# A residual block of two 3x3 convs in fp32: the far rows' products as 64 by 64 blocks on quarters of TensorE's array, and one copy of the difference sum per join

## The chip, the cores and the metric

The kernel runs on one core of one Trainium2 chip. The metric is the device time of one launch in microseconds.

## What is computed

Input x is 32 images of 64 channels, 56 by 56, in fp32. The block is a 3x3 conv, batch norm, ReLU, a second 3x3 conv, batch norm, the input added, ReLU:

```python
out = relu(_bn(_conv3x3(x, w1, stride=1), g1, b1, m1, v1))
out = _bn(_conv3x3(out, w2, stride=1), g2, b2, m2, v2)
return relu(out + identity)
```

## The kernel before, in words

**Layout.** An image is held as row pairs: 64 channels times the two rows of a pair make 128 partitions, and along the free axis stand 28 pairs by 28 even (or odd) columns. So a 128-row matmul contracts over the channels and both rows of a pair.

**Columns.** Along the columns the conv uses a transform: even and odd columns are combined into four planes, two "inner" ones (the sum and the difference of an even and an odd column, `x_inner` for the input, `t_inner` for the hidden image) and two "outer" ones (differences of columns two apart, `x_outer` and `t_outer`). Each plane is multiplied by its own filter matrix `wmat[conv][:, i]`, i = 0 to 3. Planes 1 and 2 give the sums T1 and T2 in two PSUM banks (`SUM_T1`, `SUM_T2`). The even columns are T1 + T2 + plane 0's product, the odd ones T1 - T2 + plane 3's product (banks `EVEN`, `ODD`). So after the inner products ScalarE copies T2 to `z` (`copy_sum`, L556 to 568), once plain and once negated, VectorE adds T1 to both in one instruction into `EVEN` and `ODD` (`join`, L404), and the outer products are accumulated onto that.

**Rows.** An output pair needs input rows of two neighbouring pairs. Conv 1 makes hidden pairs that are shifted by one row (`NP` = 29 of them), conv 2 turns them back. Each product is two 128x128 matrices, `far` = 0 and 1, and three of the four 64x64 blocks of each hold a filter row, the fourth is zero (`X_BLOCKS`, `HID_BLOCKS`).

**Precision.** Each product is made in three passes of the type fp32r: hi by hi, hi by lo, lo by hi, where hi is the rounded operand (ScalarE: `high_x`, `high_hidden`) and lo the rest (VectorE: `split_x`, `split_hidden`). So one product of one half image is 2 x 3 = 6 matmuls (L702). Only for images 0 and 1 some products are one fp32 matmul on the unsplit planes (`whole_passes`, operands `w_mat`).

**PSUM.** The eight banks are two halves of the image times four banks. They serve conv 1 and conv 2 in turn, with no second set.

**Steps.** The order is written out by hand, engine by engine, and kept by semaphores. In step s TensorE does, per half, conv 1's inner products of image s and conv 2's outer products of image s-2 (part A), then, per half, conv 1's outer products of image s and conv 2's inner products of image s-1 (part B), L808 to 825. VectorE's part of a step stands from L493, ScalarE's from L632. ScalarE also adds the residual into the sum banks after conv 1's join (L543), and does the two ReLUs (L573 and L608). SyncE loads and stores, GpSimd issues the accumulating load that forms the sum plane. Steps 2 to 25 run in a hardware loop of four steps.

Of the kernel before, what the change touches and what calls it, by code (L numbers as in the profile page):

```python
# [16 lines left out]
X_BLOCKS = ((0, 0, 1, 0), (0, 1, 0, 0), (0, 1, 1, 1), (1, 0, 0, 1), (1, 0, 1, 2), (1, 1, 0, 2))  # L17
HID_BLOCKS = ((0, 0, 0, 1), (0, 0, 1, 0), (0, 1, 0, 0), (1, 0, 1, 2), (1, 1, 0, 2), (1, 1, 1, 1))
OUTER = {1: {3: 0, 0: 1}, 2: {3: 0, 0: 1}}
# [7 lines left out]
def residual_block(nc, x, w1, w2, params, out):  # L27
# [4 lines left out]
    NP = NQ + 1  # L32
# [3 lines left out]

    HALF1 = ((0, (NP + 1) // 2), ((NP + 1) // 2, NP))
    HALF2 = ((0, NQ // 2), (NQ // 2, NQ))
    MAXN = HALF1[0][1] * WQ
# [5 lines left out]
    with ExitStack() as ctx:  # L45
# [8 lines left out]
        x_outer = sb("x_outer", [P, 2, RUN])  # L54
# [5 lines left out]
        t_inner = sb("t_inner", [P, 2, NP, WQ])  # L60
        t_outer = sb("t_outer", [P, 2, NP, WQ])

        ti_hi = sb("ti_hi", [P, 2, NP, WQ], F32R)
        ti_lo = sb("ti_lo", [P, 2, NP, WQ], F32R)
        h_hi = sb("h_hi", [P, 2, 2, NP, WQ], F32R)
        h_lo = sb("h_lo", [P, 2, 2, NP, WQ], F32R)
        z = sb("z", [P, 2, 2, MAXN])
        out_sb = sb("out_sb", [P, 2, 2, (NQ // 2) * WQ])

        spare = {1: z[:].rearrange("p h s r -> p (h s r)"), 2: out_sb[:].rearrange("p h s r -> p (h s r)")}  # L70
# [15 lines left out]
        w_hi = {1: sb("w1_hi", [P, 4, 2, P], F32R), 2: sb("w2_hi", [P, 4, 2, P], F32R)}  # L86
        w_lo = {1: sb("w1_lo", [P, 4, 2, P], F32R), 2: sb("w2_lo", [P, 4, 2, P], F32R)}
# [88 lines left out]
        def double_inner_filters(eng, conv, after):  # L176

            w, mat, total = w_raw[conv], wmat[conv], w_sum[conv]
            after(eng.tensor_tensor(total, w[:, 0], w[:, 2], ALU.add))
            eng.tensor_tensor(mat[:, 2], total, w[:, 1], ALU.subtract).then_inc(prep[conv], 1)  # L180
            eng.tensor_tensor(mat[:, 1], total, w[:, 1], ALU.add).then_inc(prep[conv], 1)
# [7 lines left out]
        def high_weights(conv):  # L189

            nc.scalar.wait_ge(prep[conv], 3)
            nc.scalar.wait_ge(outer_taps[conv], 1)
            nc.scalar.activation(w_hi[conv][:], wmat[conv][:], ACT.Copy).then_inc(whi_ready[conv], 1)

        def low_weights(eng, conv):

            eng.wait_ge(whi_ready[conv], 1)
            eng.tensor_tensor(w_lo[conv][:], wmat[conv][:], w_hi[conv][:].bitcast(F32),  # L198
# [10 lines left out]
        def x_full(which, k):  # L209

            full, places = (x_outer[:], slice(0, 2)) if which == "outer" else (x_inner[:, k], slice(2, 4))
# [9 lines left out]
        def hidden_rows(half):  # L221

            return slice(0, NP) if half is None else slice(*HALF1[half])

        def hidden_parts(which, b, half=None):

            rows = hidden_rows(half)
            if which != "outer":
                i = ("t1", "t2").index(which)
                return t_inner[:, i, rows], ti_hi[:, i, rows], ti_lo[:, i, rows]  # L230
            return t_outer[:, :, rows], h_hi[:, b, :, rows], h_lo[:, b, :, rows]
# [4 lines left out]

        def splits(which, n):

            return n + 1 if which == "outer" else n
# [86 lines left out]
        def _(dve):  # L326
# [19 lines left out]

            def first_x():

                dve.wait_ge(x_in[0], 16)
                cells = runs(x_sb[:, 0], 0, XPLANE + 1).rearrange("p s (j c) -> p s j c", c=WQ + 1)  # L350
                planes = x_full("inner", 0)[0]
                nc.vector.tensor_tensor(planes[:, 1], cells[:, 1, :, 0:WQ], cells[:, 0, :, 0:WQ],  # L352
                                        ALU.subtract).then_inc(tx_ready["inner"], 1)
                nc.vector.tensor_tensor(planes[:, 0], cells[:, 0, :, 0:WQ], cells[:, 1, :, 0:WQ],  # L354
                                        ALU.add).then_inc(first_sum, 1)
                cells = x_sb[:, 0, 0:2 * XPLANE].rearrange("p (s r) -> p s r", s=2)[:, :, 0:RUN] \
                    .rearrange("p s (j c) -> p s j c", c=WQ + 1)
                nc.vector.tensor_tensor(t_outer[:, :, 0:NQ], cells[:, :, :, 0:WQ], cells[:, :, :, 1:WQ + 1],  # L358
                                        ALU.subtract).then_inc(tx_ready["outer"], 1)
# [8 lines left out]
            def difference_x(n, k):  # L368
# [3 lines left out]
                cells = runs(x_sb[:, k % XBUFS], 0, XPLANE + 1).rearrange("p s (j c) -> p s j c", c=WQ + 1)  # L372
                nc.vector.tensor_tensor(x_full("inner", k)[0][:, 1], cells[:, 1, :, 0:WQ], cells[:, 0, :, 0:WQ],  # L373
                                        ALU.subtract).then_inc(tx_ready["inner"], 1)

            def outer_x(n, k):

                if is_step(n, 2):
                    dve.wait_ge(outer[1], 4)
                wait(dve, xlo_ready["outer"], n - 2)  # L380
                cells = x_sb[:, k % XBUFS]
                nc.vector.tensor_tensor(x_outer[:], runs(cells, 0, XPLANE), runs(cells, 1, XPLANE),  # L382
                                        ALU.subtract).then_inc(tx_ready["outer"], 1)
# [10 lines left out]
            def join(conv, n, half, before):  # L394

                r0, r1 = (HALF1, HALF2)[conv - 1][half]
# [6 lines left out]
                t1 = psum[:, half, SUM_T1, 0:width].unsqueeze(1).broadcast_to((P, 2, width))  # L403
# [466 lines left out]
```

## Time and profile before

| | us |
|---|---|
| median of 3 runs | 566.07 (565.9 to 566.21) |
| the profiled execution | 565.98 |
| its span | 564.3 |
| PE busy in the span | 558.4 |
| DVE busy | 542.2 |
| ACT busy | 487.2 |
| POOL busy | 30.6 |

PE is TensorE, PEld its weight loads, DVE VectorE, ACT ScalarE, POOL GpSimd, SP SyncE. The ends of matmul records are modelled and overlap the next one, so the time that a matmul takes in a stream is the distance from its start to the next start. The same holds in small for DVE and ACT, whose records overlap the next by about 0.08 us. The engine work outside of the 32 equal steps is at both ends of the kernel.

### The profile page before, as it was taken

Reading aid. Unit: us, or ns where it says so; the run is one execution under the profiler, and the core shown is the slowest. Engines: PE = TensorE matmul, PEld = TensorE weight load, DVE = VectorE, ACT = ScalarE, POOL = GpSimd, SP = SyncE. Lnnn points to the kernel's source line nnn. Section 1 sums busy time; section 2 is a strip of 40 time slices with the busy share of each in tenths; the row PEclk is TensorE's granted clock in tenths of the full one; section 3 lists DMA queues with packets and bytes.
Section 4 is the critical chain, followed back from the end, with each engine's and each line's share of the span. In section 5 each row is a group of like instructions: output and inputs, shape, how many; then the busy total and the mean of one; then the engine's idle time right before and its main releaser. Section 6 shows DMA issues by size and latency. Waiting matters only on the chain.

```text
span 564.3 us, 8999 instructions
## 1 busy us (share of the span) xinstructions
PE 558.4 (99%) x3050; PEld 543.6 (96%) x3050; DVE 542.2 (96%) x465; ACT 487.2 (86%) x744; POOL 30.6 (5%) x41
## 2 busy tenths in 40 slices
PE   8999999999999999999999999999999999999997
PEld 4689999999999999999999999999999999999997
DVE  6999999999999999999999999999999999999974
ACT  4789889888889888898888898898898988988876
POOL 3100000000000000000000000000000000000000
PEclk9999999999999999999999999999999999999999
DMA  8655445555435554445554445554355554351013
GB/s 294 180 145 145 151 109 154 148 146 165 155 91 158 159 146 151 136 120 146 174 147 143 126 138 146 149 166 151 97 158 153 146 168 142 102 154 50 30 58 114
DMA packets 31407, 79.20 MB, mean 140 GB/s; under 512 B 2592, under 2 KB 19104, under 8 KB 31392
## 3 DMA queue, kind: packets, MB, share of 16 engines
q1 hardware_dynamic: 26784, 66.05, 32.5%
q0 software_dynamic: 4464, 12.89, 14.6%
q8 instruction: 9, 0.15, 0.1%
q10 hardware_dynamic: 144, 0.07, 0.1%
q14 instruction: 6, 0.05, 0.0%
HBM read 53.31 MB, written 25.69 MB: 140 GB/s over the span
## 4 chain that ended last, share of the span: by engine, by line
PE 96%; DVE 2%; DMA 1%; issue 0%; ACT 0%; SPq 0%
PE psum L702 96%; DMA x_sb<-x_dram 1%; DVE psum L404 0%; DVE x_lo L390 0%; DVE t_outer L358 0%; DVE x_inner L352 0%; DVE x_inner L373 0%; DVE x_inner L354 0%; DVE x_outer L382 0%; DVE w_lo L198 0%; ACT out_sb L603 0%; DVE inv L332 0%; SPq L269 0%; DVE tmp L335 0%; DVE tmp L334 0%
## 5 line engine op out<-in xcount | busy, mean ns | idle before, releaser
L702 PE MATMUL psum<-x_hi,w_hi 128*128 128x420 f32 x488 | 167.2, 343 | 0.7 <-DVE x_lo L390 0.7
L702 PE MATMUL psum<-x_lo,w_hi 128*128 128x420 f32 x488 | 166.1, 340 | 0.0
L702 PE MATMUL psum<-x_hi,w_lo 128*128 128x420 f32 x488 | 166.1, 340 | 0.0
L404 DVE TENSOR_TENSOR psum<-psum,z 128x784 f32<-128x784 f32 (+1 forms) x128 | 126.9, 991 | 4.4 <-ACT z L567 4.3
L573 ACT ACTIVATE hidden<-psum,bias,half_inv 64x56 f32<-64x56 f32 (+2 forms) x128 | 84.5, 686 | 30.8 <-PE psum L702 30.3
L702 PEld LDWEIGHTS psum<-x_hi,w_hi 128*128 128x128 f32 x488 | 91.6, 188 | 2.6 <-issue 1.5
L702 PEld LDWEIGHTS psum<-x_hi,w_lo 128*128 128x128 f32 x488 | 91.7, 188 | 0.5
L702 PEld LDWEIGHTS psum<-x_lo,w_hi 128*128 128x128 f32 x488 | 91.7, 188 | 0.4
L702 PE MATMUL psum<-h_lo,w_hi 128*128 128x392 f32 x256 | 87.3, 341 | 0.0
L702 PE MATMUL psum<-h_hi,w_hi 128*128 128x392 f32 x256 | 87.3, 341 | 0.0
L702 PE MATMUL psum<-h_hi,w_lo 128*128 128x392 f32 x256 | 87.2, 341 | 0.0
L702 PE MATMUL psum<-ti_lo,w_hi 128*128 128x392 f32 x248 | 84.5, 341 | 0.0
L702 PE MATMUL psum<-ti_hi,w_hi 128*128 128x392 f32 x248 | 84.2, 340 | 0.0
L702 PE MATMUL psum<-ti_hi,w_lo 128*128 128x392 f32 x248 | 84.0, 339 | 0.0
L543 ACT ACTIVATE psum<-x_inner 128x392 f32<-128x392 f32 x128 | 58.6, 492 | 13.8 <-DVE psum L404 13.8
L608 ACT ACTIVATE out_sb<-psum 128x784 f32<-128x784 f32 x63 | 52.1, 828 | 17.3 <-PE psum L702 17.3
L441 DVE TENSOR_TENSOR ti_lo<-t_inner,ti_hi 128x812 fp32r<-128x812 f32 (+2 forms) x64 | 59.4, 970 | 0.0
L441 DVE TENSOR_TENSOR h_lo<-t_outer,h_hi 128x1624 fp32r<-128x1624 f32 (+2 forms) x33 | 59.2, 1793 | 0.0
L433 DVE TENSOR_TENSOR t_outer<-hidden 128x1624 f32<-128x1624 f32 (+2 forms) x33 | 59.1, 1790 | 0.0
L382 DVE TENSOR_TENSOR x_outer<-x_sb 128x1624 f32<-128x1624 f32 x31 | 57.1, 1842 | 0.0
L553 ACT ACTIVATE ti_hi<-t_inner 128x812 fp32r<-128x812 f32 (+2 forms) x64 | 55.8, 875 | 0.4 <-DVE t_inner L414 0.3
L390 DVE TENSOR_TENSOR x_lo<-x_inner,x_hi 128x1568 fp32r<-128x1568 f32 x31 | 55.4, 1786 | 0.0
(66 smaller groups left out, 806.3 us busy)
## 6 DMA issues: line engine op xcount, KB each, us to landing
x_sb<-x_dram SPq DMA_DIRECT2D x32, 814.0 KB, 5.0
out_dram<-out_sb SPq DMA_DIRECT2D x63, 392.0 KB, 2.8
x_inner<-x_dram SPq DMA_DIRECT2D x31, 406.0 KB, 3.2
x_inner<-x_dram POOLq DMA_DIRECT2D x31, 406.0 KB, 5.2
out_dram<-out_sb SPq DMA_DIRECT2D x2, 196.0 KB, 2.3
z<-w_dram SPq DMA_DIRECT2D x1, 384.0 KB, 3.7
out_sb<-w_dram SPq DMA_DIRECT2D x1, 384.0 KB, 6.3
bn<-params_dram ACTq DMA_DIRECT2D x1, 68.0 KB, 3.9
```

The lines of the kernel that those rows point to most:

```text
L382: nc.vector.tensor_tensor(x_outer[:], runs(cells, 0, XPLANE), runs(cells, 1, XPLANE), ALU.subtract).then_inc(tx_ready["outer"], 1)
L390: nc.vector.tensor_tensor(x_part(x_lo, k, places), full, x_part(x_hi, k, places).bitcast(F32), ALU.subtract).then_inc(xlo_ready[which], 1)
L404: nc.vector.tensor_tensor(psum[:, half, EVEN:ODD + 1, 0:width], t1, z[:, half, :, 0:width], ALU.add).then_inc(joined[conv], 1)
L433: nc.vector.tensor_tensor(t_outer[:, :, rows], hid_cols[:, :, rows, 0:WQ], hid_cols[:, :, rows, 1:WQ + 1], ALU.subtract).then_inc(th_ready ...
L441: nc.vector.tensor_tensor(lo, full, hi.bitcast(F32), ALU.subtract).then_inc(hlo_ready[which], 1)
L543: ins = nc.scalar.activation(psum[:, half, bank, 0:width].rearrange("p (j q) -> p j q", q=WQ), x_full("inner", k)[0][:, i, j0:j1], ACT.Cop ...
L553: nc.scalar.activation(hi, full, ACT.Copy).then_inc(hhi_ready[which], 1)
L573: return nc.scalar.activation(hid_data[rows, :, pairs, 0:WQ], sums[rows], ACT.Relu, bias=bias[rows, 0:1], scale=half_inv[rows, 0:1])
L608: nc.scalar.activation(out_sb[:, half], psum[:, half, EVEN:ODD + 1, 0:(j1 - j0) * WQ], ACT.Relu).then_inc(out_ready, 1)
L702: ins = nc.tensor.matmul(sums, w[:, i, far, :], t[:, j0:j1, 0:WQ], start=not onto and at == 0, stop=at == len(todo) - 1, skip_group_check= ...
```

## The change

**Rows.** The shift is gone: hidden pairs are the same as input pairs (`NP` = 28, halves of 14 pairs for both convs, 392 columns). Of the 3x3 filter's row products of a pair, four 64x64 blocks stay within the pair and fill one 128x128 matrix without a zero (`pair_products`). Two blocks reach into a neighbour pair: each is now a matmul of its own with 64 rows and 64 columns of weights (`near_products`), on 392 columns, or 364 at the image's edge. The output rows of conv 1 are swapped within a pair (`X_BLOCKS`), so its two blocks cross from partitions 0-63 to 64-127 and back, while those of conv 2 stay in their half. `near_rows` puts conv 1's and conv 2's blocks behind each other at the end of each half of part A and of part B.

**Precision.** Pair products stay in three fp32r passes for conv 1 and for conv 2's outer planes. Conv 2's inner pair products are one fp32 matmul each, and so are all the near blocks. The splits `ti_hi`, `ti_lo` of the hidden image's inner planes and their buffers are gone; `t_inner`, `t_outer` and `x_outer` get a second buffer.

**Joins.** `copy_sum` copies T2 once. `join` is two instructions, T1 + z into `EVEN` and T1 - z into `ODD`. Conv 2's bias moves from `copy_sum` to the last ReLU. The residual is two ACT instructions of 64 partitions with 784 elements instead of two of 128 with 392. `relu_hidden` is one instruction of 784 instead of two.

```diff
-            def sum_products(conv, half, i, bank, passes, onto):
...
-                todo = [(far, t, w) for far in (whole, 1 - whole) for t, w in passes]
...
+            def pair_products(conv, half, i, bank, k, native):
...
+                if native:
+                    passes = ((plane(conv, i, k), wmat[conv][:, i, 0]),)
...
+                    passes = ((hi, w_hi[conv][:, i]), (hi, w_lo[conv][:, i]), (lo, w_hi[conv][:, i]))
+                fresh = conv == 1 and i in (1, 2)
+                for at, (t, w) in enumerate(passes):
+                    ins = nc.tensor.matmul(sums, w, t[:, r0:r1, 0:WQ], start=fresh and at == 0,
+                                           stop=at == len(passes) - 1, skip_group_check=True)
...
+            def near_products(conv, half, i, bank, k):
+
+                r0, r1 = HALVES[half]
+                for source, shift in ((0, 1), (1, -1)):
+
+                    j0, j1 = max(r0, -shift), min(r1, NQ - shift)
+                    rows = slice(source * C, source * C + C)
+                    place = 1 - source if conv == 1 else source
+                    out = slice(place * C, place * C + C)
...
+                    ins = nc.tensor.matmul(sums, wmat[conv][rows, i, 1, out],
+                                           plane(conv, i, k)[rows, j0 + shift:j1 + shift], start=False, stop=True,
+                                           skip_group_check=True)
...
+            def near_rows(half, of_inner=None, of_outer=None):
+
+                for i, bank, o, target in ((2, SUM_T2, 0, EVEN), (1, SUM_T1, 3, ODD)):
+                    if of_inner:
+                        conv, k = of_inner
+                        near_products(conv, half, i, bank, k).then_inc(inner[conv], 1)
+                    if of_outer:
+                        conv, k = of_outer
+                        ins = near_products(conv, half, o, target, k)
...
-                t1 = psum[:, half, SUM_T1, 0:width].unsqueeze(1).broadcast_to((P, 2, width))
-                nc.vector.tensor_tensor(psum[:, half, EVEN:ODD + 1, 0:width], t1, z[:, half, :, 0:width],
-                                        ALU.add).then_inc(joined[conv], 1)
...
+                for bank, op in ((EVEN, ALU.add), (ODD, ALU.subtract)):
+                    ins = nc.vector.tensor_tensor(psum[:, half, bank, 0:width], psum[:, half, SUM_T1, 0:width],
+                                                  z[:, half, 0:width], op)
+                ins.then_inc(joined[conv], 1)
...
-                for i, bank, share in ((0, SUM_T1, 0.5), (1, SUM_T2, -0.5)):
-                    ins = nc.scalar.activation(psum[:, half, bank, 0:width].rearrange("p (j q) -> p j q", q=WQ),
-                                               x_full("inner", k)[0][:, i, j0:j1], ACT.Copy, scale=share)
+                for source, target in ((slice(C, P), slice(0, C)), (slice(0, C), slice(C, P))):
+                    sums = psum[target, half, SUM_T1:SUM_T2 + 1, 0:width].rearrange("p s (j q) -> p s j q", q=WQ)
+                    ins = nc.scalar.activation(sums, x_full("inner", k)[0][source, :, j0:j1], ACT.Copy, scale=0.5)
...
-                if conv == 1:
-                    nc.scalar.activation(z[:, half, 0, 0:width], t2, ACT.Copy)
-                    ins = nc.scalar.activation(z[:, half, 1, 0:width], t2, ACT.Copy, scale=-1.0)
...
+                ins = nc.scalar.activation(z[:, half, 0:width], t2, ACT.Copy)
```

The engines' rows in the steady state. First PE, part A of the first half in the loop, before: conv 2's outer products of image s-2, whose two matrices have six passes per plane (`h_hi` and `h_lo` are the split outer planes of the hidden image).

```order
L702 MATMUL psum<-h_hi,w_hi 128x392 [waits joined2,hlo_outer]
L702 MATMUL psum<-h_hi,w_lo 128x392
L702 MATMUL psum<-h_lo,w_hi 128x392
L702 MATMUL psum<-h_hi,w_hi 128x392
L702 MATMUL psum<-h_hi,w_lo 128x392
L702 MATMUL psum<-h_lo,w_hi 128x392
L702 MATMUL psum<-h_hi,w_hi 128x392
L702 MATMUL psum<-h_hi,w_lo 128x392
L702 MATMUL psum<-h_lo,w_hi 128x392
L702 MATMUL psum<-h_hi,w_hi 128x392
L702 MATMUL psum<-h_hi,w_lo 128x392
L702 MATMUL psum<-h_lo,w_hi 128x392
```

In the changed kernel the same place has six passes for both planes (the last four stand here), and then the eight 64-row matmuls of `near_rows`, two of conv 1 (`x_inner`) and two of conv 2 (`t_outer`) in turn.

```order
L651 MATMUL psum<-h_lo,w_hi 128x392
L651 MATMUL psum<-h_hi,w_hi 128x392
L651 MATMUL psum<-h_hi,w_lo 128x392
L651 MATMUL psum<-h_lo,w_hi 128x392
L665 MATMUL psum<-x_inner,w_mat 64x392
L665 MATMUL psum<-x_inner,w_mat 64x364
L665 MATMUL psum<-t_outer,w_mat 64x392
L665 MATMUL psum<-t_outer,w_mat 64x364
L665 MATMUL psum<-x_inner,w_mat 64x392
L665 MATMUL psum<-x_inner,w_mat 64x364
L665 MATMUL psum<-t_outer,w_mat 64x392
L665 MATMUL psum<-t_outer,w_mat 64x364
```

Of the twelve passes six are left, and eight fp32 matmuls of a quarter of the array each end the half. The signal that conv 1's sums are complete now comes from among these eight.

Then DVE, before: a step of the loop from conv 2's join of the second half (image s-2) to conv 1's join of the second half (image s). L404 is the join, L390 the split of an x plane, L441 that of a hidden plane.

```order
L404 TENSOR_TENSOR psum<-psum,z 128x2x392 [waits hidden_ready,inner2,z2_ready]
L433 TENSOR_TENSOR t_outer<-hidden 128x1624 [waits hlo_outer]
L390 TENSOR_TENSOR x_lo<-x_outer,x_hi 128x1568 [waits xhi_outer]
L399 ISA
L400 ISA [waits z1_ready]
L404 TENSOR_TENSOR psum<-psum,z 128x2x420 [waits out_ready,inner1]
L441 TENSOR_TENSOR ti_lo<-t_inner,ti_hi 128x812 [waits hhi_t1]
L441 TENSOR_TENSOR ti_lo<-t_inner,ti_hi 128x812 [waits hhi_t2]
L441 TENSOR_TENSOR h_lo<-t_outer,h_hi 128x1624 [waits hhi_outer]
L399 REGISTER_ALU
L400 ISA [waits z1_ready]
L404 TENSOR_TENSOR psum<-psum,z 128x2x392 [waits out_ready,inner1]
```

The same stretch after, up to the hidden image's split; L393 is the join, L379 and L420 are the splits.

```order
L379 TENSOR_TENSOR x_lo<-x_outer,x_hi 128x1568 [waits xhi_outer]
L393 TENSOR_TENSOR psum<-psum,z 128x392 [waits hidden_ready,inner2,z2_ready]
L393 TENSOR_TENSOR psum<-psum,z 128x392
L144 REGISTER_ALU [waits hidden_ready]
L401 TENSOR_TENSOR t_inner<-hidden 128x784 [waits inner2]
L412 TENSOR_TENSOR t_outer<-hidden 128x1568 [waits outer2]
L388 ISA
L389 ISA [waits z1_ready]
L393 TENSOR_TENSOR psum<-psum,z 128x392 [waits out_ready,inner1]
L393 TENSOR_TENSOR psum<-psum,z 128x392
L406 TENSOR_TENSOR t_inner<-hidden 128x784
L420 TENSOR_TENSOR h_lo<-t_outer,h_hi 128x1568 [waits hhi_outer]
```

The split of the outer x plane moved from behind the hidden image's planes to ahead of conv 2's join, the two splits of `t_inner` are gone, the difference of the hidden columns moved behind conv 1's first join, and each join is two rows.

## Rows read from the trace of the kernel before

**Rows 1.** Section 1 of the page: busy time, share of the span, instructions.

```profile
PE 558.4 (99%) x3050; PEld 543.6 (96%) x3050; DVE 542.2 (96%) x465; ACT 487.2 (86%) x744; POOL 30.6 (5%) x41
```

**Rows 2.** Section 2 of the page: the granted clock in 40 slices.

```profile
PEclk9999999999999999999999999999999999999999
```

**Rows 3.** Windows: busy time of each engine (x instructions), 100 to 500 us.

```profile
100.00:500.00 400.00, 400.00 (x2245) 399.12 (x2244) 395.49 (x329) 354.32 (x539) 20.70 (x24) 1.00 0.50 146
```

**Rows 4.** The chain that ended last: start us, us, what.

```profile
19.22 542.00 PE psum L702 x3008
...
561.25 0.50 ACT out_sb L603
```

**Rows 5.** Timeline of DVE: start us, us, engine, line, operation, tiles, forms.

```profile
290.37 0.96 DVE L373 TENSOR_TENSOR x_inner<-x_sb 128x784 f32<-128x784 f32 x1
...
300.51 1.84 DVE L441 TENSOR_TENSOR h_lo<-t_outer,h_hi 128x1624 fp32r<-128x1624 f32 x1
302.27 0.97 DVE L404 TENSOR_TENSOR psum<-psum,z 128x784 f32<-128x784 f32 x1
303.16 1.84 DVE L382 TENSOR_TENSOR x_outer<-x_sb 128x1624 f32<-128x1624 f32 x1
304.91 1.78 DVE L390 TENSOR_TENSOR x_lo<-x_inner,x_hi 128x1568 fp32r<-128x1568 f32 x1
306.62 0.98 DVE L404 TENSOR_TENSOR psum<-psum,z 128x784 f32<-128x784 f32 x1
307.50 0.96 DVE L373 TENSOR_TENSOR x_inner<-x_sb 128x784 f32<-128x784 f32 x1
308.65 1.00 DVE L414 TENSOR_TENSOR t_inner<-hidden 128x812 f32<-128x812 f32 x1 [0.19 <-PE psum L702]
309.58 1.00 DVE L421 TENSOR_TENSOR t_inner<-hidden 128x812 f32<-128x812 f32 x1
...
341.72 0.97 DVE L373 TENSOR_TENSOR x_inner<-x_sb 128x784 f32<-128x784 f32 x1
```

**Rows 6.** Timeline of PE: twelve three-pass matmuls in the steady state.

```profile
302.15 0.34 PE L702 MATMUL psum<-ti_hi,w_hi 128*128 128x392 f32 x1
...
304.10 0.34 PE L702 MATMUL psum<-ti_lo,w_hi 128*128 128x392 f32 x1
304.28 0.34 PE L702 MATMUL psum<-x_hi,w_hi 128*128 128x392 f32 x1
```

**Rows 7.** Groups by form, PE: count | busy us, mean ns of one.

```profile
L702 PE MATMUL psum<-ti_hi,w_hi 128*128 128x392 f32 x248 | 84.2, 340 | 0.0
...
L702 PE MATMUL psum<-t_inner,w_mat 128*128 128x392 f32 x16 | 5.6, 492 | 0.0
```

**Rows 8.** Timeline of PE: fp32 matmuls without splits, early in the kernel.

```profile
26.29 2.80 PE L702 MATMUL psum<-t_inner,w_mat 128*128 128x392 f32 x8
28.92 2.71 PE L702 MATMUL psum<-x_outer,w_mat 128*128 128x392 f32 x8
```

**Rows 9.** Timeline of DVE, near the end: the 392-element forms.

```profile
550.25 0.56 DVE L414 TENSOR_TENSOR t_inner<-hidden 128x392 f32<-128x392 f32 x1
550.72 0.56 DVE L421 TENSOR_TENSOR t_inner<-hidden 128x392 f32<-128x392 f32 x1
```

**Rows 10.** Groups by form, ACT.

```profile
L543 ACT ACTIVATE psum<-x_inner 128x392 f32<-128x392 f32 x128 | 58.6, 492 | 13.8 <-DVE psum L404 13.8
L553 ACT ACTIVATE ti_hi<-t_inner 128x812 fp32r<-128x812 f32 x60 | 53.8, 897 | 0.4 <-DVE t_inner L414 0.3
L608 ACT ACTIVATE out_sb<-psum 128x784 f32<-128x784 f32 x63 | 52.1, 828 | 17.3 <-PE psum L702 17.3
L573 ACT ACTIVATE hidden<-psum,bias,half_inv 64x56 f32<-64x56 f32 x64 | 25.0, 391 | 30.4 <-PE psum L702 30.3
```

**Rows 11.** Timeline of PEld: weight loads while PE stands idle.

```profile
19.19 0.19 PEld L702 LDWEIGHTS psum<-x_hi,w_hi 128*128 128x128 f32 x1 [1.29 <-issue]
19.30 0.19 PEld L702 LDWEIGHTS psum<-x_hi,w_lo 128*128 128x128 f32 x1
```

More of the change, by code:

```diff
@@ L209, in x_full @@
         def x_full(which, k):
-            full, places = (x_outer[:], slice(0, 2)) if which == "outer" else (x_inner[:, k], slice(2, 4))
+            full, places = (x_outer[:, k % 2], slice(0, 2)) if which == "outer" else (x_inner[:, k], slice(2, 4))
             return full.rearrange("p s (j c) -> p s j c", c=WQ + 1)[:, :, :, 0:WQ], places
@@ L219, in until, with hidden_outer @@
             return (n - k % 2) * 8 + 16
[L221 to L231, printed above, removed]
+        def hidden_outer(b):
+            return t_outer[:, b], h_hi[:, b], h_lo[:, b]
         def split_of_x(which, n):
             return n - 1 if which == "outer" else n
-        def splits(which, n):
-            return n + 1 if which == "outer" else n
         def before_conv2(n):
@@ L653, in step @@
                     copy_sum(2, 0, 1)
+                    high_x("outer", 2, 2)
                     return
-                if now:
-                    high_x("outer", s, k)
-                if last:
-                    high_hidden("t1", s - 1, kl % 2)
+                if ahead:
+                    high_x("inner", s + 1, ka)
+                if there_is(s, s - 2):
+                    relu_out(s - 2, 0)
                 if now:
@@ L676, in step @@
                 if last:
-                    residual(s - 1, kl, 1)
                     copy_sum(2, s - 1, 0)
+                if ahead:
+                    high_x("outer", s + 1, ka)
                 if now:
@@ L747, in outer_products, with inner_pairs_1, outer_pairs @@
+            def inner_pairs_1(half, k, native=False):
+                for i, bank in ((2, SUM_T2), (1, SUM_T1)):
+                    pair_products(1, half, i, bank, k, native)
+            def outer_pairs(conv, n, half, k, native=False):
                 pe.wait_ge(joined[conv], 2 * n + half + 1)
                 for i, bank in ((0, EVEN), (3, ODD)):
-                    first = conv == 1 and (is_step(n, 0) or is_step(n, 1))
-                    passes = whole_passes(1, i, n) if first else passes_of(conv, i, b)
@@ L751, in outer_products, with inner_pairs_2 @@
-                    ins = sum_products(conv, half, i, bank, passes, True)
-                    if conv == 2 and half == 1 and is_step(n, N - 1):
-                        ins.then_inc(last_bank, 1)
-                if not (conv == 2 and half == 1 and is_step(n, N - 1)):
-                    ins.then_inc(outer[conv], 1)
+                    pair_products(conv, half, i, bank, k, native)
+            def inner_pairs_2(n, half, k):
+                pe.wait_ge(th_ready["t1"], n + 1)
+                pe.wait_ge(th_ready["t2"], n + 1)
+                pe.wait_ge(res_ready, 2 * n + half + 1)
+                for i, bank in ((2, SUM_T2), (1, SUM_T1)):
+                    pair_products(2, half, i, bank, k, True)
```

335 lines of the change are left out of this document (136 added, 199 removed).

## The prediction

> **What bounds the kernel now.** I read the page's first two sections, a window of the steady state, the chain, and then timelines. PE is busy for 99% of the span and DVE for 96% [rows 1], and the chain is 542.0 us of matmuls without a break, from 19.22 us to the last ReLU [rows 4]. The granted clock stays at its upper level, 2.4 GHz [rows 2, 3]. Between 100 and 500 us PE is never idle and DVE is busy 395.5 of 400 us, ACT 354.3 [rows 3]. So two engines are close to full, and ACT is not far behind. The same DVE operation starts at 290.37 and, three steps later, at 341.72 [rows 5]: a step (one image) takes 17.12 us. 32 steps are 547.8 us, and the other 16.5 us of the span lie at its ends. The profiled execution took 565.98 us, 1.7 us more than its span and 0.1 under the median, so I add 1.7 to a span.
>
> **Part 1, fewer three-pass matmuls.** Twelve of them start between 302.15 and 304.28 [rows 6]: 0.1775 us each for 392 columns. A step had 96; 36 are left (conv 1's four planes and conv 2's two outer ones, two halves, three passes). 36 x 0.1775 = 6.4 us.
>
> **Part 2, conv 2's inner pairs in fp32.** Four fp32 matmuls of 392 columns appear as eight records and take 28.92 - 26.29 = 2.63 us [rows 8], so 0.657 us each, as two records of 0.329. (Three passes would be 0.53.) Four per step: 2.6 us.
>
> **Part 3, the near blocks.** A step has four calls of `near_rows` with eight matmuls of 64 rows by 64 columns each, in fp32. The trace has no matmul on part of the array, so I bound a call. If four run at once, one in each quarter, a call is two rounds of the full-size fp32 matmul, 2 x 0.657 = 1.31 us. If none overlap it is 8 x 0.657 = 5.26 us. Cheaper than 1.31 would need a matmul to take less than its columns did in rows 8, and nothing in the program makes them fewer. I take 1.31: the two blocks of conv 1 and the two of conv 2 use the four different quarters, stand behind each other, and depend on nothing of each other. Four calls: 5.3 us.
>
> **Part 4, changing between whole array and quarters.** Eight changes a step. A three-pass matmul's record lasts 340 ns [rows 7] while the next starts after 177.5 [rows 6], so some 0.165 us of each lies over its successor. If the array has to run empty at a change, that overlap is lost: 8 x 0.165 = 1.3 us. The other end is 0. The Trainium skill, TensorEngine Tiling (Array Packing), Key Properties, says that changing the tiling mode drains TensorE. By that rule the 1.3 us are real; if it did not hold PE's sum would be 43 us lower (rival D); no row here shows a change.
>
> I take 0.165, the only size that the rows give for an emptying pipe.
>
> PE's step: 6.4 + 2.6 + 5.3 + 1.3 = **15.6 us**.
>
> **Part 5, DVE.** By distances of starts [rows 5]: x split 1.71, `x_outer` 1.75, join of 784 elements 0.89, a hidden plane of 812 elements 0.93 (0.89 for 784, by the join), and `x_inner` 0.88 (its record less 0.08). 392 elements take 0.47 from SBUF [rows 9]; I take 0.48 for them from PSUM (the joins of 784 run 0.01 longer than `x_inner` of 784). New step: `x_inner` 0.88, `x_outer` 1.75, two x splits, `t_outer` and `h_lo` of 1568 elements each 4 x 1.71, sum and difference 2 x 0.89, eight half joins 8 x 0.48 = 3.84. Together 15.1 us, where it was about 16.9 [rows 3]. The splits of `t_inner` go (-1.8), the joins grow by 0.3. DVE alone would give 32 x 15.1 + 16.5 + 1.7 = 501 us.
>
> **Part 6, ACT.** From 15.2 us a step (354.3 us over 23.4 steps [rows 3]) go two `ti_hi` of 0.90, the two short ReLUs of 0.39, and four z copies, about 0.49 each by the residual's form of the same 392 elements [rows 10]; the residual's four instructions of 784 elements are put at 0.83 (the last ReLU's 784 elements, [rows 10]) to 1.0 us instead of 0.49, +1.4 to +2.0. That leaves 12 to 12.6 us. ACT does not bound; the removed ACT work is worth nothing by itself. Smaller edits (half the weight splits at the start, the bias in the last ReLU) lie beside matmuls or DVE's start; the load requests keep their waits and only come 1.5 us closer together, with the DMA engines half busy [rows 3]. I cost them at nothing.
>
> **The sum over the whole kernel,** since one-conv calls at the ends fill only two quarters. Everything before 19.2 us stays: image 0's fp32 matmuls and near blocks have the same total as the two full matrices had (16 x 0.657 against 8 x 0.657 + 4 x 1.31). Behind it: 1116 three-pass matmuls, 198.1; 132 fp32 ones, 86.7; the equivalent of 130 near calls, 170.8; 262 changes, 43.2; together 498.8. With 19.2 ahead and the last ReLU's 0.5 the span is 518.5, and the time **520 us**.
>
> **Where it is tight.** The waits go around through the single set of PSUM banks. From the start of a step DVE now needs 0.88 + 1.71 + 0.96 = 3.55 us to finish conv 2's second join, and PE asks for it after 12 x 0.1775 + 1.31 + 0.33 = 3.77. Conv 1's first join ends at 3.55 + 0.89 + 1.71 + 0.96 = 7.1, PE asks at 7.5; the residual on ACT behind it (two of at least 0.75 by distance of starts) ends at 8.6, and PE's next inner pair asks at 7.5 + 1.07 = 8.6. Behind a late join stand DVE's splits, and on PE, behind the waiting pair, the near blocks that release both convs' sums. So a slower residual is seen at once: 0.5 us a step is 16 us. I put nothing into the point for it and 25 us into the range.
>
> **Rivals.**
>
> *A. The quarters run only two at a time (0.16).* Each fp32 matmul is two records [rows 7, 8] and the second needs the same quarter as the first. If matmuls start strictly in the order of the program, the next block's first half can only start with this block's second half: 16 records become 8 slots of 0.329, a call 2.63 us instead of 1.31. 122 two-conv calls lie behind 19.2 us: 122 x 1.31 = +160, **680 us**, slower. For it: no row shows PE starting matmuls out of order. Against: no row shows it starting two together either, so the rows are silent. The Trainium skill, TensorEngine Tiling (Array Packing), PSUM Pressure, gives another way to the same time: row tiles must not use one PSUM bank at the same time, and the two blocks of a `near_products` do write one bank (on different partitions); they would then go one after the other, beside the other conv's, which is again two at a time. The break-even for all such cases: 46 us over 122 calls, so a two-conv call with its changes of 2.0 us, where I have 1.64.
>
> *B. Nothing overlaps (0.04).* 122 x (5.26 - 1.31) = +482, and +10 from the one-conv calls: about 1010 us.
>
> *C. The weight loads set the pace of the near rows (0.05).* With PE idle two loads start 0.11 us apart [rows 11]. A call has 16 loads; at 0.11 each, if a load of 64 columns costs as much as one of 128 and cannot hide, it takes 1.76 us instead of 1.31: +55, 575 us, slower.
>
> *D. The changes cost nothing, and DVE sets the pace (0.12).* PE's step is 14.3, DVE's 15.1: 501 us. A DVE between two engines rarely runs without a gap, so some more is as likely.
>
> *E. The waits of the tight places add 0.8 to 1.4 us a step (0.14).* 545 to 565 us, with PE idle before `t_inner` or the outer pairs.
>
> **Chances.** The forecast, 505 to 545 us, has 0.48; D 0.12 and E 0.14 are faster than before as well. Within 0.2% (1.1 us, about what a measurement of this kernel can tell from no change): 0.01. Slower: A 0.16, B 0.04, C 0.05. So faster 0.74, same 0.01, slower 0.25. The range takes in D, E and C, 498 to 590 us, and leaves out A and B. For the likeliest sign alone it is 498 to 560.
>
> **What would show it.** Right: 64-row matmuls that start within some tens of ns of each other, four abreast, a call near 1.3 us, a gap of 0.1 to 0.2 us at each change; a step of 15.5 to 15.8; DVE busy 97% with eight joins of about 0.56 us; ACT near 80%. A is right if 64-row records start 0.33 us apart. C if weight loads are back to back with matmuls spaced behind them. D if the changes leave no gap and PE waits for joins. E if PE is idle ahead of `t_inner` with ACT's residual as the releaser. The forecast is wrong if a call with its changes is over 2.0 us, or if the step is over 17.1 us for any reason.

## The result and the profile after

The changed kernel takes 547.41 us (median of 4 runs, 547.39 to 547.64) against 566.0 us in the same session: a ratio of 0.967, 95% interval 0.966 to 0.969. It is 18.6 us faster. The forecast was 520 us, 46 us faster. The gain is 0.4 of that one; the time lies in the stated range, 498 to 590 us, and 2.4 us above the forecast's own 505 to 545 us.

The page, section 1, of the changed kernel, to be laid beside [rows 1]:

```profile
PE 531.8 (97%) x3454; PEld 317.6 (58%) x3454; DVE 486.0 (89%) x525; ACT 412.4 (76%) x487; POOL 30.1 (6%) x41
```

The windows view of the changed kernel, the steady state (busy time and instructions of PE, PEld, DVE, ACT, POOL; granted clock, DMA share, GB/s), to be laid beside [rows 3]:

```profile
100.00:500.00 400.00, 396.88 (x2674) 242.99 (x2674) 374.28 (x398) 317.54 (x372) 20.76 (x24) 1.00 0.51 149
```

All three engines do less. Yet no engine is full for 400 us any more: PE is idle for 3 us and DVE for 26. The length of a step is read from the timeline of DVE, from `x_outer` to `x_outer`, 21 steps apart:

```profile
99.18 1.84 DVE L344 TENSOR_TENSOR x_outer<-x_sb 128x1624 f32<-128x1624 f32 x1
...
439.30 1.84 DVE L344 TENSOR_TENSOR x_outer<-x_sb 128x1624 f32<-128x1624 f32 x1
```

340.12 / 21 = 16.20 us a step, where it was 17.12 and 15.6 was forecast. (The steps behind the hardware loop, from 26 on, are a little shorter, 16.04 us.) So 30 steps (2 to 31) cost some 17 us more than forecast, and the other 10 us lie at the ends.

The near rows do what they say. Timeline of PE in the changed kernel, part A of a first half, from its first whole-array matmul through one call of `near_rows` to the next whole-array one:

```profile
298.53 0.45 PE L651 MATMUL psum<-x_hi,w_hi 128*128 128x392 f32 x1
...
300.59 0.33 PE L651 MATMUL psum<-h_lo,w_hi 128*128 128x392 f32 x1
300.85 0.54 PE L665 MATMUL psum<-x_inner,w_mat 64*64 64x392 f32 x2
300.86 0.54 PE L665 MATMUL psum<-t_outer,w_mat 64*64 64x392 f32 x2
301.21 0.47 PE L665 MATMUL psum<-x_inner,w_mat 64*64 64x364 f32 x1
301.23 0.47 PE L665 MATMUL psum<-t_outer,w_mat 64*64 64x364 f32 x1
301.23 0.49 PE L665 MATMUL psum<-x_inner,w_mat 64*64 64x392 f32 x1
301.24 0.49 PE L665 MATMUL psum<-t_outer,w_mat 64*64 64x392 f32 x1
...
302.32 0.45 PE L651 MATMUL psum<-x_hi,w_hi 128*128 128x392 f32 x1
```

Four records start within some 0.03 us (the row marked x2 holds two of them), the next four some 0.3 us later, and so on: four rounds, sixteen records. From 300.85 to 302.32 is 1.47 us. A whole first half of part A takes 302.32 - 298.53 = 3.79 us; the forecast's terms for it (12 x 0.1775 + 1.31 + 0.33) give 3.77.

What the forecast did not have is the gap on DVE. Timeline of DVE in the changed kernel over the same stretch:

```profile
302.46 1.78 DVE L412 TENSOR_TENSOR t_outer<-hidden 128x1568 f32<-128x1568 f32 x1
304.20 1.05 DVE L393 TENSOR_TENSOR psum<-psum,z 128x392 f32<-128x392 f32 x2
305.15 0.96 DVE L406 TENSOR_TENSOR t_inner<-hidden 128x784 f32<-128x784 f32 x1
306.04 1.78 DVE L420 TENSOR_TENSOR h_lo<-t_outer,h_hi 128x1568 fp32r<-128x1568 f32 x1
308.88 1.05 DVE L393 TENSOR_TENSOR psum<-psum,z 128x392 f32<-128x392 f32 x2 [1.06 <-ACT z L531]
309.84 1.84 DVE L344 TENSOR_TENSOR x_outer<-x_sb 128x1624 f32<-128x1624 f32 x1
```

Timeline of ACT in the changed kernel beside it:

```profile
304.27 1.51 ACT L522 ACTIVATE h_hi<-t_outer 128x1568 fp32r<-128x1568 f32 x1 [0.40 <-DVE t_outer L412]
305.81 1.66 ACT L513 ACTIVATE psum<-x_inner 64x784 f32<-64x784 f32 x2
307.41 0.89 ACT L557 ACTIVATE out_sb<-psum,bias 128x784 f32<-128x784 f32 x1
308.21 0.48 ACT L531 ACTIVATE z<-psum 128x392 f32<-128x392 f32 x1
```

ACT waits for `t_outer`, rounds it, and only then makes the residual, the output ReLU of the second half and the copy of T2. DVE's second join of conv 1 waits for that copy, and everything of DVE stands behind it, the next step's `t_outer` too. From one `t_outer` back to it that is a ring. Its ACT part takes 4.42 us (from 304.27 to 308.69), and the DVE work beside it, a join, a difference and a split, only 3.62 (from 304.20 to 307.82).

### The profile page after: what moved, and what is told of

It is laid out like the page before. It is cut to its first block, busy times and chain, and to the rows that moved or that the text cites. A ratio compares the mean times of both kernels' runs of the same rounds, so it can differ in the third digit from the quotient of the medians.

```text
span 545.8 us, 9539 instructions
## 1 busy us (share of the span) xinstructions
PE 531.8 (97%) x3454; PEld 317.6 (58%) x3454; DVE 486.0 (89%) x525; ACT 412.4 (76%) x487; POOL 30.1 (6%) x41
## 4 chain that ended last, share of the span: by engine, by line
DVE 44%; PE 24%; issue 16%; ACT 13%; DVEq 1%; ACTq 0%; POOL 0%; POOLq 0%
PE psum L651 14%; DVE psum L393 12%; PE psum L665 9%; DVE x_lo L379 9%; DVE t_outer L412 8%; DVE x_outer L344 7%; ACT psum L513 6%; DVE t_inner L401 4%; ACT out_sb L557 4%; DVE x_inner L338 3%; ACT z L531 2%; PE psum L705 1%; ACT h_hi L522 1%; DVEq L144 1%; DVE h_lo L420 0%
## 5 line engine op out<-in xcount | busy, mean ns | idle before, releaser
L393 DVE TENSOR_TENSOR psum<-psum,z 128x392 f32<-128x392 f32 x256 | 133.2, 565 | 42.8 <-ACT z L531 38.9
L513 ACT ACTIVATE psum<-x_inner 64x784 f32<-64x784 f32 x128 | 105.5, 824 | 39.0 <-DVE psum L393 37.4
L651 PE MATMUL psum<-t_inner,w_mat 128*128 128x392 f32 x256 | 99.3, 510 | 7.7 <-ACT psum L513 5.9
L665 PE MATMUL psum<-t_outer,w_mat 64*64 64x392 f32 (+1 forms) x512 | 98.4, 491 | 0.0
L665 PE MATMUL psum<-x_inner,w_mat 64*64 64x392 f32 (+1 forms) x512 | 98.0, 490 | 0.0
L665 PE MATMUL psum<-x_outer,w_mat 64*64 64x392 f32 (+1 forms) x512 | 98.0, 490 | 0.0
L665 PE MATMUL psum<-t_inner,w_mat 64*64 64x392 f32 (+1 forms) x512 | 98.0, 490 | 0.0
L651 PE MATMUL psum<-x_hi,w_hi 128*128 128x392 f32 x244 | 95.9, 393 | 1.9 <-DVE psum L393 1.9
L651 PE MATMUL psum<-x_hi,w_lo 128*128 128x392 f32 x244 | 83.0, 340 | 0.0
L651 PE MATMUL psum<-x_lo,w_hi 128*128 128x392 f32 x244 | 82.8, 339 | 0.0
L420 DVE TENSOR_TENSOR h_lo<-t_outer,h_hi 128x1568 fp32r<-128x1568 f32 x32 | 57.0, 1782 | 1.6 <-ACT h_hi L522 1.6
L379 DVE TENSOR_TENSOR x_lo<-x_outer,x_hi 128x1568 fp32r<-128x1568 f32 x30 | 53.5, 1783 | 2.0 <-ACT x_hi L502 2.0
L379 DVE TENSOR_TENSOR x_lo<-x_inner,x_hi 128x1568 fp32r<-128x1568 f32 x31 | 55.3, 1783 | 0.0
```

Of the source, the lines that this page charges most:

```text
L379: nc.vector.tensor_tensor(x_part(x_lo, k, places), full, x_part(x_hi, k, places).bitcast(F32), ALU.subtract).then_inc(xlo_ready[which], 1)
L393: ins = nc.vector.tensor_tensor(psum[:, half, bank, 0:width], psum[:, half, SUM_T1, 0:width], z[:, half, 0:width], op)
L420: nc.vector.tensor_tensor(lo, full, hi.bitcast(F32), ALU.subtract).then_inc(hlo_ready["outer"], 1)
L513: ins = nc.scalar.activation(sums, x_full("inner", k)[0][source, :, j0:j1], ACT.Copy, scale=0.5)
L651: ins = nc.tensor.matmul(sums, w, t[:, r0:r1, 0:WQ], start=fresh and at == 0, stop=at == len(passes) - 1, skip_group_check=True)
L665: ins = nc.tensor.matmul(sums, wmat[conv][rows, i, 1, out], plane(conv, i, k)[rows, j0 + shift:j1 + shift], start=False, stop=True, skip_g ...
```

## Experiments

Each run is set beside the kernel before (565.7 to 565.8 us in these sessions). "Step" is the mean over 17 to 21 steps, read as above. Line numbers move by a few lines between the kernels.

**1. The near blocks conv by conv.**

```diff
-                for i, bank, o, target in ((2, SUM_T2, 0, EVEN), (1, SUM_T1, 3, ODD)):
-                    if of_inner:
+                if of_inner:
+                    for i, bank in ((2, SUM_T2), (1, SUM_T1)):
                         conv, k = of_inner
                         near_products(conv, half, i, bank, k).then_inc(inner[conv], 1)
-                    if of_outer:
+                if of_outer:
+                    for o, target in ((0, EVEN), (3, ODD)):
                         conv, k = of_outer
                         ins = near_products(conv, half, o, target, k)
-                if of_outer:
                     ins.then_inc(outer[of_outer[0]], 1)
```

> The near blocks of the two convs no longer alternate: in each call conv by conv, so at most two quarters have work at a time. Theory T (four quarters really work at once, and PE's own work sets the step): each two-conv call grows from two to four rounds of an fp32 matmul, 1.31 us; 120 calls in the steps: about +155 us, some 703 us. Rival R1 (the four abreast records are only how the profile draws them, and PE works through them at two at a time in any order): no change, 547 us. Rival R2 (DVE and ACT's ring of waits sets the step, PE has slack): less than half of T's, under 625 us.

548.26 us, step 16.21: no change. Theory T's premise, that this order leaves work for two quarters only, was wrong. Timeline of PE in this run, one call:

```profile
302.01 0.54 PE L665 MATMUL psum<-x_inner,w_mat 64*64 64x392 f32 x2
302.04 0.54 PE L665 MATMUL psum<-t_outer,w_mat 64*64 64x392 f32 x2
302.38 0.51 PE L665 MATMUL psum<-x_inner,w_mat 64*64 64x364 f32 x2
302.40 0.51 PE L665 MATMUL psum<-t_outer,w_mat 64*64 64x364 f32 x2
...
303.50 0.45 PE L651 MATMUL psum<-x_hi,w_hi 128*128 128x392 f32 x1
```

`t_outer`'s first block starts 0.03 us after `x_inner`'s, although four blocks of `x_inner` stand ahead of it in the program: a quarter that is free takes its matmul from further back. So this run does not take the four-abreast work apart. It gives rival R1's number too, and R1 stays open until run 2, which does take it apart.

**2. The near blocks of each conv behind its own pairs, in part A.**

```diff
                         inner_pairs_1(half, k)
+                        near_rows(half, (1, k), None)
...
-                        near_rows(half, (1, k) if now else None, (2, kb) if store else None)
+                        if store:
+                            near_rows(half, None, (2, kb))
```

> In part A of each half conv 1's near blocks stand directly behind conv 1's pair products, and conv 2's behind conv 2's: whole-array matmuls lie between, so only two quarters can have work, and there are 4 more changes a step. If a call of one conv takes as long as one of two convs (1.47 us from its first matmul to the next whole-array one in the changed kernel's trace) plus 0.18 us for the extra changes, PE's part A grows by 1.65 us a half: 2 x 1.65 x 30 = 99, less the 0.25 us a step that PE stands now: about 638 us. If four abreast are no faster than two, so that a one-conv call takes half: 555 us, like the run with more changes.

630.73 us, ratio 1.115 (1.113 to 1.117), step 19.02: 2.8 us more a step (638 us was expected; R1's like here was 555). Timeline of PE, a call with one conv's blocks alone:

```profile
304.41 1.53 PE L665 MATMUL psum<-x_inner,w_mat 64*64 64x392 f32 x8
305.87 0.45 PE L651 MATMUL psum<-h_hi,w_hi 128*128 128x392 f32 x1
```

Half the blocks take 1.46 us, as long as all of them. The second conv's blocks in a call are free. This is what rival A denied, shown by its price: with two quarters at work in part A alone, the kernel would be slower than before.

**3. More changes between whole array and quarters, in part A.**

```diff
-                        inner_pairs_1(half, k)
...
-                        outer_pairs(2, s - 2, half, kb)
+                        pe.wait_ge(joined[2], 2 * (s - 2) + half + 1)
...
-                        near_rows(half, (1, k) if now else None, (2, kb) if store else None)
+                        for i, bank, o, target in ((2, SUM_T2, 0, EVEN), (1, SUM_T1, 3, ODD)):
+                            if now:
+                                pair_products(1, half, i, bank, k, False)
+                            if store:
+                                pair_products(2, half, o, target, kb, False)
+                            if now:
+                                near_products(1, half, i, bank, k).then_inc(inner[1], 1)
+                            if store:
+                                ins = near_products(2, half, o, target, kb)
+                        if store:
+                            ins.then_inc(outer[2], 1)
```

> Part A of each half makes the same matmuls, but the near blocks in two lots, each behind the pair products of its own planes: 4 more changes between whole array and quarters, and 4 fewer stretches of a full length between them, per step. If a change costs the 0.165 us of the prediction and PE sets the step, 4 x 0.165 x 30 = +20 us, 567 us. If it costs 0.24 (the measured PE step of 15.9 us less 14.3, over 8 changes, less what else may be in it: an upper figure), +24 to +29, up to 576 us. If changes are free and the rest of PE's step has another cause, 547 us. If the ring of DVE and ACT sets the step, also near 547 us.

555.25 us, ratio 0.982 (0.980 to 0.984), step 16.44. Timeline of PE, the first half of part A, with four changes in it instead of two:

```profile
301.73 0.45 PE L651 MATMUL psum<-x_hi,w_hi 128*128 128x392 f32 x1
...
305.88 0.45 PE L651 MATMUL psum<-x_hi,w_hi 128*128 128x392 f32 x1
```

4.15 us against 3.79 for two changes more: 0.18 us a change. The forecast's 0.165 was right in size. The kernel grew by less (8 us instead of 20), which says that PE's own work was not what set the step of 16.20.

**4. No near blocks.**

```diff
-                    pair_products(1, half, i, bank, k, native)
+                    pair_products(1, half, i, bank, k, native).then_inc(inner[1], 1)
...
             def near_rows(half, of_inner=None, of_outer=None):
+                return
```

The other pair products raise their semaphores in the same way. The output lacks the neighbour pairs' part.

> All near blocks are left out (the output lacks each output pair's contribution from the neighbour pair), with their changes; the semaphores are raised by the pair products. PE's step is then 6.4 + 2.6 = 9.0 us. It shows the step of DVE and ACT alone. DVE's work is 15.1 us a step. If DVE can run without gaps: 32 x 15.1 + 16.5 + 1.7 = about 501 us. If the ring of waits (single set of PSUM banks) sets a floor near the measured step of 16.2 even with a fast PE: 535 to 547 us. In between: waits remain, but PE's own work is the larger part of the loss.

537.56 us. The step, from the same rows of DVE, 19 steps apart:

```profile
111.09 1.84 DVE L344 TENSOR_TENSOR x_outer<-x_sb 128x1624 f32<-128x1624 f32 x1
...
418.97 1.84 DVE L344 TENSOR_TENSOR x_outer<-x_sb 128x1624 f32<-128x1624 f32 x1
```

(418.97 - 111.09) / 19 = 16.20 us, the same as with them, though PE is now busy for 215 of 320 us (window 100 to 420). And DVE has the same gap ahead of the same join:

```profile
304.58 1.05 DVE L393 TENSOR_TENSOR psum<-psum,z 128x392 f32<-128x392 f32 x2 [1.11 <-ACT z L531]
```

So in the changed kernel DVE and ACT set the step, by their order; PE is just short of it. The 10 us that this run is faster lie at the ends. (With PE idle that often, its granted clock was 0.974 and 0.958 in the two executions, 536.53 and 538.6 us. PE does not set the step here: run 9 below, with PE as idle and a clock of 1.00 in this window, again has the step of the kernel with near blocks.)

**5. The ring shortened.** Run 4's kernel, and one of the residual's two instructions left out.

```diff
-                for source, target in ((slice(C, P), slice(0, C)), (slice(0, C), slice(C, P))):
+                for source, target in ((slice(C, P), slice(0, C)),):
```

> The changed kernel's order, without near blocks, and with one of the residual's two instructions left out (the output lacks the neighbour pairs' contributions and the input on half of the rows). The run without near blocks kept the step of 16.20 us. Theory T2 (ring: DVE t_outer, ACT rounding, two residual instructions, output ReLU, copy of T2, DVE join, and then DVE without a gap to the next t_outer): one instruction less on ACT, 0.80 us by distance of starts, takes 0.8 us from every step: 15.4 us, about 512 us. Rival (the residual lies beside the ring, which runs through the copy or the rounding alone): 16.2 us, 537 us.

513.53 us, step 15.48: 0.72 us less a step for an instruction of 0.80. The residual is in the ring. That is where the change's own form of it counts: two instructions of 64 partitions and 784 elements take 1.66 us. In a timeline of ACT before, two of 128 by 392 take 0.92:

```profile
298.81 0.92 ACT L543 ACTIVATE psum<-x_inner 128x392 f32<-128x392 f32 x2 [0.52 <-DVE psum L404]
```

Each instruction now has twice the elements on half of the partitions. What the old form would give in the changed kernel was not run.

**6. The joins alone, on the kernel before.**

```diff
+                for bank, op in ((EVEN, ALU.add), (ODD, ALU.subtract)):
+                    ins = nc.vector.tensor_tensor(psum[:, half, bank, 0:width], psum[:, half, SUM_T1, 0:width],
+                                                  z[:, half, 0, 0:width], op)
...
-                if conv == 1:
-                    nc.scalar.activation(z[:, half, 0, 0:width], t2, ACT.Copy)
-                    ins = nc.scalar.activation(z[:, half, 1, 0:width], t2, ACT.Copy, scale=-1.0)
...
+                ins = nc.scalar.activation(z[:, half, 0, 0:width], t2, ACT.Copy)
...
-                                     ACT.Relu).then_inc(out_ready, 1)
+                                     ACT.Relu, bias=bias[:, 1:2]).then_inc(out_ready, 1)
```

> The kernel before with only one part of the change: the difference sum copied once, each join as an addition and a subtraction, conv 2's bias in the last ReLU. ACT loses four copies a step (about 1.6 us by distance of starts), DVE's joins grow by 0.06 us each, four a step, so 16.9 + 0.25 = 17.15 us against a step of 17.12. Theory T (the part helps ACT only, which does not bound): 566 to 572 us. Rival: ACT's copies were on the ring of waits, so a shorter ACT gives some time back: 560 to 565 us.

566.36 us, ratio 1.0011 (1.0002 to 1.0021). Window of this run:

```profile
100.00:500.00 400.00, 400.00 (x2245) 399.11 (x2244) 400.00 (x424) 316.00 (x445) 20.71 (x24) 1.00 0.49 146
```

ACT falls from 354 to 316 us and nothing comes of it; DVE rises from 395.5 to 400. This part of the change gives no time by itself, as forecast; it makes room on ACT, which the new residual takes.

**7. ACT's order in steps 1 and N.**

```diff
+                    residual(N - 1, kl, 1)
                     high_hidden(N - 1, kl % 2)
-                    residual(N - 1, kl, 1)
...
                     high_x("inner", 2, 2)
+                    residual(0, 0, 1)
                     high_hidden(0, 0)
                     relu_hidden(1, 0)
-                    residual(0, 0, 1)
                     copy_sum(2, 0, 0)
+                    high_x("outer", 2, 2)
                     relu_hidden(1, 1)
                     copy_sum(2, 0, 1)
-                    high_x("outer", 2, 2)
```

> Only ScalarE's order in steps 1 and N is changed: in step 1 the second residual goes ahead of the hidden image's rounding and the rounding of image 2's outer x planes goes ahead of the last hidden ReLU; in step N the second residual goes ahead of the rounding. In the changed kernel's trace PE stands for 1.63 us before the second inner pairs of conv 2, 1.92 us before conv 1 of image 2, and 0.93 us in the tail. Theory (these waits are on the path that sets the end): up to 4.5 us less, 543 to 545 us. Rival: the waits only move on to the next join: no change, 547 us.

544.33 us, ratio 0.962 (0.961 to 0.964): 3.1 us of the 4.5. So about a third of the 10 us that the ends cost more was order.

**8. The ring's order in every step.** On top of run 7:

```diff
                 if last:
                     difference_hidden(s - 1, kl % 2)
-                    split_hidden(s - 1, kl % 2)
+                if ahead:
+                    outer_x(s + 1, ka)
                 if now:
                     join(1, s, 1, (2, s - 2))
+                if last:
+                    split_hidden(s - 1, kl % 2)
                 if ahead:
-                    outer_x(s + 1, ka)
                     split_x("inner", s + 1, ka)
...
                 if last:
-                    high_hidden(s - 1, kl % 2)
                     residual(s - 1, kl, 0)
...
                     copy_sum(1, s, 1)
                 if last:
+                    high_hidden(s - 1, kl % 2)
                     residual(s - 1, kl, 1)
```

The first piece is DVE's order, the second ACT's.

> The order of e5, and in every step of the loop: ScalarE makes the residual, the output ReLU and the copy of T2 ahead of the rounding of the hidden outer planes; VectorE makes the next image's x_outer ahead of conv 1's second join and the split of the hidden planes behind it. Same instructions. Theory T2 (the ring DVE t_outer, ACT rounding, residual, output ReLU, copy, DVE join sets the step at 16.2 us, as the run without near blocks showed, and DVE's gap of 1.06 to 1.11 us a step is that ring): the gap shrinks, and PE's own 15.95 us set the step: about 7 us less than e5, 536 to 539 us. Rival R3 (PE with its changes sets the step as much): less than 3 us under e5. Rival R4 (the ring only moves, for the split of the hidden planes now comes later): 547 us or more.

534.92 us, ratio 0.946 (0.944 to 0.947), step 15.86: 9.4 us under run 7 from the same instructions. The gap ahead of the join is now 0.47 us, and PE is busy for all 400 us of its window.

**9. The same order without near blocks.** Run 8's kernel with the edit of run 4.

> The order of e6 with all near blocks left out (the output lacks the neighbour pairs' contributions), so PE's step is some 9 us and the step is what DVE and ACT need. Theory T2: DVE's 15.1 us of work bound it, 15.1 to 15.4 us a step: 505 to 515 us. Rival R4 (the ring only moved): a step of 16 us or more, over 530 us.

527.62 us and a step of 15.86 again. Both theories missed: the ring had shortened by 0.35 us and still was no shorter than PE's own step. In the gap DVE waits behind `x_outer` for ACT's residual, ReLU and copy. Timeline of DVE in run 9:

```profile
314.36 1.05 DVE L393 TENSOR_TENSOR psum<-psum,z 128x392 f32<-128x392 f32 x2 [0.47 <-ACT z L533]
315.59 1.79 DVE L420 TENSOR_TENSOR h_lo<-t_outer,h_hi 128x1568 fp32r<-128x1568 f32 x1 [0.19 <-ACT h_hi L524]
```

**10. More DVE work between conv 1's two joins.** On top of run 8 the sum of the hidden columns moves behind the first join.

```diff
-                    sum_hidden(s - 1, kl % 2)
+                    dve.wait_ge(hidden_ready, 2 * (s - 1) + 2)
                     outer_hidden(s - 1, kl % 2)
                 if now:
                     join(1, s, 0, (2, s - 2))
                 if last:
+                    sum_hidden(s - 1, kl % 2)
                     difference_hidden(s - 1, kl % 2)
```

> The order of e6, and DVE's sum of the hidden columns moved behind conv 1's first join, so that DVE has 3.5 us of its own work between conv 1's two joins instead of 2.6 (the chain on ACT between them is about 3.1). Same instructions. If in e6 the ring alone sets the step of 15.86 us, it falls with the ring, to 15.5 or so: 524 to 530 us. If PE's own work of some 15.9 us sets it as well (its window of 400 us had no idle time), the time stays at 534 to 536 us.

533.52 us, ratio 0.943 (0.941 to 0.944), step 15.85 in the loop.

**11. The same order without near blocks.** Run 10's kernel with the edit of run 4.

> e10 with all near blocks left out (the output lacks the neighbour pairs' contributions): what DVE and ACT alone need a step in that order. If the move shortens the ring: 15.1 to 15.5 us a step, 505 to 518 us. If the gap only moves to another join: 15.86 us, 527 us.

501.93 us, step 15.01. The windows view of run 10:

```profile
100.00:420.00 320.00, 320.00 (x2184) 199.55 (x2188) 304.95 (x325) 256.95 (x303) 18.12 (x21) 1.00 0.52 157
```

The same window of run 11:

```profile
100.00:420.00 320.00, 226.77 (x939) 161.16 (x937) 320.00 (x342) 266.14 (x320) 18.13 (x21) 0.99 0.55 164
```

In run 11 DVE is busy for all of 320 us: its own work is 15.0 us a step, and the ring no longer adds to it. So in run 10, where PE is full, it is PE that sets the step of 15.85. Behind the loop PE is as full, and run 10's step is shorter. Timeline of DVE in run 10, four steps apart:

```profile
424.89 1.84 DVE L344 TENSOR_TENSOR x_outer<-x_sb 128x1624 f32<-128x1624 f32 x1
...
487.78 1.84 DVE L344 TENSOR_TENSOR x_outer<-x_sb 128x1624 f32<-128x1624 f32 x1
```

62.89 / 4 = 15.72 us. Run 10 is the fastest complete kernel here, 32 us under the kernel before and 14 under the changed one, with the changed one's instructions in another order.

## Why the prediction was right or wrong

*What held.* Four quarters work at once (part 3): 1.47 us for a call with its last change, and run 2 for the price of losing it. Rivals A and B are out, and so is C, by the same 1.47 us against its 1.76 without a change; weight loads of neighbouring quarters start together, as the records do (300.85 and 300.86). A change costs 0.18 us in run 3 (part 4: 0.165), so rival D is out as well. The Trainium skill, TensorEngine Tiling (Array Packing), Key Properties, has a drain at a change of mode; run 3 agrees, with 0.18 us. DVE's own step is 15.0 us in run 11 (part 5: 15.1) and the work taken off ACT is worth nothing by itself (part 6, run 6). ACT's step is 12.9 us (317.54 of 400 us), a little over the 12 to 12.6 of part 6. The rule of the same page of the Trainium skill, PSUM Pressure, that row tiles cannot use one bank at the same time, does not hold for this kernel. Timeline of PE in the changed kernel:

```profile
297.41 0.47 PE L665 MATMUL psum<-t_inner,w_mat 64*64 64x364 f32 x1
297.42 0.47 PE L665 MATMUL psum<-x_outer,w_mat 64*64 64x364 f32 x1
297.44 0.49 PE L665 MATMUL psum<-t_inner,w_mat 64*64 64x392 f32 x1
297.45 0.49 PE L665 MATMUL psum<-x_outer,w_mat 64*64 64x392 f32 x1
```

The two records of `t_inner` are the two blocks of one product. They read different halves of the partitions, write one bank on different partitions, and start 0.03 us apart; taking turns, they would need the 2.63 us a call of rival A, and it takes 1.47.

*What failed first: "I put nothing into the point for it", the waits of the tight places.* The prediction found the tight places and then took all waits as nothing, because each sum of durations just fitted PE's clock. It had left out what stands around the residual in ACT's queue. The residual does not stand directly behind conv 1's first join; the rounding `h_hi` stands ahead of it, which waits for `t_outer`. And the second join needs the copy, which stands behind the residual and the output ReLU. Counted as it stands in the order, ACT's part is 1.5 + 1.6 + 0.8 + 0.5 = 4.4 us, and DVE has only 3.6 us to put beside it. The difference, 0.8 us, and the hand-overs from DVE to ACT and back (0.07 us before 304.27, 0.19 behind 308.69) are DVE's gap of 1.06 us, and 15.1 + 1.1 = 16.2 is the step. Two busy engines that hand work to each other in fixed order have a period of their own; "PE 15.6, DVE 15.1, so 15.6" skipped it. Runs 4 and 5 show it, and runs 8 and 10 take it away: 16.20 - 15.85 = 0.35 us a step, some 10 us. Rival E had the right time (545 to 565) and the residual as a culprit, but its time is in part luck: it put 0.8 to 1.4 us of waits into each step, where they cost 0.35, and the rest of the miss came from PE's own step and the ends. Its sign is there, but small: the page has PE idle for 7.7 us ahead of `t_inner`, 5.9 of it by the residual. PE is nearly as slow as the ring, and a record's modelled end hides some 0.16 us of each wait.

*What failed second: PE's step, 15.85 instead of 15.6,* 7 us over 30 steps. One half of it is the price of a change (part 4). With 0.18 instead of 0.165 for each of the eight, PE's terms give 15.7, and run 10 has 15.72 behind the loop. The prices of parts 1 to 3 hold. Timeline of PE in run 10 there, the two fp32 pair products of a half of part B:

```profile
441.38 1.48 PE L654 MATMUL psum<-t_inner,w_mat 128*128 128x392 f32 x4
442.78 0.54 PE L668 MATMUL psum<-t_inner,w_mat 64*64 64x392 f32 x2
```

They take 1.40 us: 2 x 0.657 = 1.31 and the change into quarters, 0.09 (in part A the last whole-array matmul takes 300.85 - 300.59 = 0.26 instead of 0.1775). The other half is 0.13 us that only the steps in the loop have. In the changed kernel's loop the same two products take

```profile
311.68 1.58 PE L651 MATMUL psum<-t_inner,w_mat 128*128 128x392 f32 x4
313.19 0.55 PE L665 MATMUL psum<-t_inner,w_mat 64*64 64x364 f32 x2
```

1.51 us, and in run 10's loop one of the two pairs of a step takes 1.48. What makes them longer in the loop stays open.

*Third, the ends, 10 us.* 3.1 are waits behind ACT's order (run 7). 2.4 are the last store: the sum over the whole kernel ended with the last ReLU, but in the changed kernel that ends at 543.4 and the span at 545.8 us. It was inside the 16.5 us of the step-wise sums, and got lost when the prediction changed to the other way of summing. 0.5 are image 0: its changes were not counted, and the matmuls behind it start at 19.69 instead of 19.2. The other 4 us were not traced.

Together 10 + 7 + 10 = 27 us, which is the miss.

## What to carry to other kernels

When two engines are both near full and wait for each other, write down the ring between them, every queued instruction included, before taking the larger sum of work as the period; the sum of the durations around it is a third candidate beside the two engines. Leaving out one engine's work altogether (here PE's near rows) tells in one run which of the three sets the step. And after a change that moves work between engines, the order of the queues is worth another look: here it held back 14 us that the change had already paid for.

## What was not expected of the hardware

A free quarter of TensorE's array takes a matmul from behind others that wait for their quarter. In run 1 `t_outer`'s first block, eight records behind `x_inner`'s first, started 0.03 us after it, and a call took 303.50 - 302.01 = 1.49 us against 1.47 in alternating order. So the alternation in `near_rows` is not what buys the overlap. What buys it is that both convs' blocks stand in one stretch, without a whole-array matmul between them (run 2: 1.46 us for half of the blocks).
